# A decoder layer on one core: the order of work in the feed-forward rows, and where the first row's second stage starts

## The reference

```python
# 1: linear attention, 16 heads of 128, blocks of 64 with decay per head
qkv = silu(x @ Wqkv.T);  q, k, v = split(qkv)
out = blockwise_decayed_attention(q, k, v, slope_rate)   # = masked scores with exp(-s*(i-j))
rms = rsqrt(mean(out * out, axis=-1) + eps)              # over all heads, 2048 features
attn = sigmoid(x @ Wg.T) * (out * rms * norm_w) @ Wo.T
x1 = layernorm(x + attn)

# 2: a recurrence over the 256 steps, per feature; k = x1, v = ctx
#    y_t = (a_t + exp(u + k_t) * v_t) / (b_t + exp(u + k_t))
#    a' = exp(w) * a + exp(k_t) * v_t ;  b' = exp(w) * b + exp(k_t) ,  w = -exp(time_decay)
x2 = layernorm(x1 + y)

# 3: feed-forward with ternary weights, 512 -> 2048 -> 512
h = bitlinear(x2, w_fc); h = gelu(h); h = bitlinear(h, w_proj)
return layernorm(x2 + h)
```

## Time and profile before

| | |
|---|---|
| median of 3 runs | 1429.16 us |
| lowest to highest | 1429.12 to 1431.48 us |
| the profiled execution | 1429.61 us |
| its span (first to last instruction) | 1427.20 us |
| PE busy | 1353.2 us (95%) |
| weight load (PEld) busy | 1056.6 us (74%) |
| DVE busy | 961.6 us (67%) |
| ACT busy | 621.6 us (44%) |
| POOL busy | 268.5 us (19%) |
| mean granted clock of TensorE | 0.986 |

### The profile page before, as it was taken

The page is one execution under the profiler, slowest core; times in us unless marked ns, Lnnn a source line. Parts: engine busy times, 40 slices in busy tenths (PEclk is TensorE's granted clock), DMA queues, the critical chain, the costliest instruction groups (busy, mean ns, idle before and its releaser), DMA issues. The chain is left out here.

```text
span 1427.2 us, 21094 instructions
## 1 busy us (share of the span) xinstructions
PE 1353.2 (95%) x6898; PEld 1056.6 (74%) x6898; DVE 961.6 (67%) x1712; ACT 621.6 (44%) x1182; POOL 268.5 (19%) x199
## 2 busy tenths in 40 slices
PE   7999999998999999999999999999995789998897
PEld 6888888887888888888888888888883344454443
DVE  5666666655666657667666766555658788888873
ACT  5433434342434343433434343434331667767754
POOL 2210101110101011110101110101113454444430
PEclk9999999999999999999999999999997899999999
DMA  5011111110111010110101010000000001111000
GB/s 199 5 46 54 59 37 59 47 63 23 45 37 44 22 44 22 46 44 28 44 22 44 22 44 8 30 7 29 28 24 17 30 30 45 44 44 45 15 16 29
DMA packets 14435, 55.00 MB, mean 39 GB/s; under 512 B 2112, under 2 KB 2112, under 8 KB 12096
## 3 DMA queue, kind: packets, MB, share of 16 engines
q1 hardware_dynamic: 14400, 54.55, 11.2%
HBM read 50.35 MB, written 4.19 MB: 38 GB/s over the span
## 5 line engine op out<-in xcount | busy, mean ns | idle before, releaser
L333 PE MATMUL bank<-x_hi,w_hi 128*128 128x512 f32 x1024 | 413.3, 404 | 7.9 <-DVE x_lo L859 7.1
L335 PE MATMUL bank<-x_hi,w_lo 128*128 128x512 f32 x1024 | 401.1, 392 | 0.0
L334 PE MATMUL bank<-x_lo,w_hi 128*128 128x512 f32 x1024 | 400.1, 391 | 0.0
L844 DVE TENSOR_TENSOR resid<-resid,bank 128x512 f32<-128x512 f32 x256 | 173.6, 687 | 149.7 <-PE bank L384 148.7
L1252 POOL TENSOR_TENSOR sq_sum<-sq_sum,o_sq 128x512 f32<-128x512 f32 x64 | 104.8, 1637 | 872.2 <-ACT o_sq L604 872.2
L333 PEld LDWEIGHTS bank<-x_hi,w_hi 128*128 128x128 f32 x1024 | 193.1, 189 | 47.5 <-issue 9.1
L335 PEld LDWEIGHTS bank<-x_hi,w_lo 128*128 128x128 f32 x1024 | 192.9, 188 | 42.8
L334 PEld LDWEIGHTS bank<-x_lo,w_hi 128*128 128x128 f32 x1024 | 193.5, 189 | 36.7
L850 DVE SCALAR_TENSOR_TENSOR gated<-g_t,bank 128x512 f32<-128x512 f32 x64 | 44.0, 687 | 176.2 <-PE bank L364 176.2
L599 ACT ACTIVATE v_t<-bank 128x512 f32<-128x512 f32 x64 | 38.2, 596 | 185.9 <-PE bank L335 185.9
L382 PE MATMUL bank<-wo_hi,u_hi 128*128 128x512 f32 x256 | 100.8, 394 | 14.6 <-DVE u_lo L855 14.3
(11 more groups left out here) (147 smaller groups left out, 2401.6 us busy)
## 6 DMA issues: line engine op xcount, KB each, us to landing
w_raw<-w_ffn SPq DMA_DIRECT2D x32, 512.0 KB, 3.3
raw<-w_heads SPq DMA_DIRECT2D x15, 1024.0 KB, 4.9
raw<-w_heads SPq DMA_DIRECT2D x17, 256.0 KB, 2.7
x_in<-x_rows SPq DMA_DIRECT2D x8, 512.0 KB, 3.3
val<-ctx_t SPq DMA_DIRECT2D x8, 512.0 KB, 3.3
out<-y_out SPq DMA_DIRECT2D x8, 512.0 KB, 2.6
resid<-x_t SPq DMA_DIRECT2D x3, 1024.0 KB, 9.3
resid<-x_t SPq DMA_DIRECT2D x4, 256.0 KB, 5.2
```

Source lines behind the costliest of these rows:

```text
L333: mm(PJ[j % 2][:, :], a, c, start=kt == 0, stop=False)
L334: mm(PJ[j % 2][:, :], a, d, start=False, stop=False)
L335: last = mm(PJ[j % 2][:, :], b, c, start=False, stop=kt == KT - 1)
L844: tt(resid[:, 4 * g + t, :], resid[:, 4 * g + t, :], YB[t % 2][:, :], ALU.add).then_inc(y_added, 1)
```

## The change

On each engine the same instructions are issued, with these differences:

- In `row` DVE does both reciprocals before the aa scans, and these behind the first half-split; `input_sum` moves from the middle of the row (for row b+2) to its end (for row b+3), so that it stands ahead of the next bb scans. GpSimd does den ahead of the two products, and the root for the input norm at the row's start. `second_stats` is no longer behind `input_sum`.
- The scans have 255 columns in place of 256, over tiles of 256, since the last state was not read.
- `final` moves one unit ahead, to unit 62. In unit 63 PE turns row 0's x1 into the scores' banks, ACT copies the key and takes the exponentials between its key and value evacuations (two more table loads), DVE does the bb scans ahead of `gate(62)`, and GpSimd den and the products.
- Behind unit 63 row 0 takes the path of the others (`invert`, `fraction` on GpSimd) and `first_fraction` goes. PE does the column sums before the mix and `turn_back(0)` before the last outputs.
- The tiles of the rows lie in another order.

```diff
-            def unit(h, g, lag1=True, lag2=True, fresh=False, final=False):
+            def unit(h, g, lag1=True, lag2=True, fresh=False, final=False, turn=False):
...
                 project(h, g, K)
+                if turn:
+                    pe.wait_ge(masked, 2 * u)
+                    turn_x1(0, SC)
...
             U = UNITS
+            pe.wait_ge(key_ok, 2)
             scores(U - 1, 0)
             scores(U - 1, 1)
-            pe.wait_ge(evacuated, PROJ * U)
-            turn_x1(0)
             for tt in range(4):
                 output(HEADS - 1, U - 2, tt)
+            column_sums()
             mix(U - 1)
-            for tt in range(4):
+            pe.wait_ge(evacuated, PROJ * U)
+            turn_back(0)
+            for tt in range(2):
                 output(HEADS - 1, U - 1, tt)
+            pe.wait_ge(col_ok, 1)
+            turn_x2(0, 0)
+            for tt in range(2, 4):
+                output(HEADS - 1, U - 1, tt)
+            turn_x1(1, TR)
             pe.wait_ge(sq_added, U)
             pe.wait_ge(v_ready, U)
             square_totals(1, GROUPS)
-            column_sums()
-            turn_back(0)
-            pe.wait_ge(col_ok, 1)
-            turn_x2(0, 0)
-            turn_x1(1)
...
                     evacuate(u, j)
+                    if j == K and first_row:
+                        split_k(u)
+                        copy_key(0, SC)
+                        act.wait_ge(bias_ok, 2)
+                        exps(0)
+                        continue
...
             def row(b, first=False, next_row=True, second_row=True):
-                if next_row:
+                if second_row:
+                    root(NX, b + 2)
+                if next_row:
+                    denominator(b + 1)
                     weighted(b + 1)
-                    denominator(b + 1)
-                    numerator(b + 1)
                 if not first:
                     root(NO, b - 1)
                 if next_row:
+                    numerator(b + 1)
                     fraction(b + 1, 0)
                     fraction(b + 1, 1)
-                if second_row:
-                    root(NX, b + 2)
...
             root(NX, 0)
+            add_squares(UNITS - 3, 1)
+            pool.wait_ge(projected, PROJ * (UNITS - 1))
+            g_.memset(bb[:, :, 0:1], 1.0).then_inc(states0, 1)
+            denominator(0)
+            pool.wait_ge(wo_split, HEADS)
+            weighted(0)
             add_squares(UNITS - 2, GROUPS - 2)
-            pool.wait_ge(projected, PROJ * UNITS)
-            g_.memset(bb[:, :, 0:1], 1.0).then_inc(states0, 1)
-            weighted(0)
             numerator(0)
+            fraction(0, 0)
+            fraction(0, 1)
+            root(NX, 1)
+            second_root(0)
             add_squares(UNITS - 1, GROUPS - 1)
             rms_root(1, GROUPS)
-            second_root(0)
-            root(NX, 1)
```

More of the change, by code:

```diff
@@ L391, in square_totals, with turn_x1 @@
                 last.then_inc(sq_total, 1)
-            def unit(h, g, lag1=True, lag2=True, fresh=False, final=False):
+            def turn_x1(b, to):
+                pe.wait_ge(x1_ok, BT * b + BT)
+                wait(pe, x2_ok, BT * b)
+                for ct in range(KT):
+                    for t in range(BT):
+                        o = (ct % 2) * SEQ + t * P
+                        last = nc.tensor.transpose(to[ct // 2][:, o:o + P], x1[:, t, ct * P:(ct + 1) * P],
+                                                   ident[:, :])
+                last.then_inc(x1_turned, 1)
+            def unit(h, g, lag1=True, lag2=True, fresh=False, final=False, turn=False):
                 u = GROUPS * h + g
@@ L434, in _ @@
             for g in range(GROUPS):
[L435 to L445, removed]
+                unit(HEADS - 1, g, final=g == GROUPS - 2, turn=g == GROUPS - 1)
             def turn_back(b):
@@ L623, in copy_v, with copy_key, exps, unit @@
                 fn(v_r[:, :, :], VT[:, :].rearrange("p (a b) -> p a b", a=KT), ACT.Copy).then_inc(v_ready, 1)
-            def unit(h, g, lag1=True, split=None):
+            def copy_key(b, turned):
+                act.wait_ge(x1_turned, b + 1)
+                wait(act, r_ok, 2 * b)
+                for c in range(2):
+                    fn(key[:, 2 * c:2 * c + 2, :], turned[c][:, :].rearrange("p (a b) -> p a b", a=2),
+                       ACT.Copy).then_inc(key_ok, 1)
+            def exps(b):
+                act.wait_ge(key_ok, 2 * b + 2)
+                wait(act, num_ok, b)
+                for c in range(KT):
+                    fn(ek1[:, c, :], key[:, c, :], ACT.Exp, bias=u_neg[:, c:c + 1]).then_inc(ek1_ok, 1)
+                for c in range(KT):
+                    fn(ek2[:, c, :], key[:, c, :], ACT.Exp, bias=u_min[:, c:c + 1]).then_inc(ek2_ok, 1)
+            def unit(h, g, lag1=True, split=None, first_row=False):
                 u = GROUPS * h + g
@@ L661, in _ @@
             for g in range(GROUPS):
[L662 to L677, removed]
-                    fn(ek2[:, c, :], key[:, c, :], ACT.Exp, bias=u_min[:, c:c + 1]).then_inc(ek2_ok, 1)
+                unit(HEADS - 1, g, first_row=g == GROUPS - 1)
             def split_x2(b):
@@ L914, in head @@
                 for g in range(GROUPS):
-                    unit(h, g, final=last and g == GROUPS - 1)
+                    unit(h, g, final=last and g == GROUPS - 2, first_row=last and g == GROUPS - 1)
                     if g == 1:
@@ L1186, in _ @@
             gate(U - 1)
-            first_fraction()
+            scale_columns()
+            input_sum(1)
+            second_stats(0)
+            root = second_shift(0)
+            shift(NX, 1)
+            fc_scale(0, root)
+            for t in range(2):
+                add_y(U - 1, (U - 1) % GROUPS, t)
+            split_x2(0)
             for t in range(2, 4):
@@ L1266, in _ @@
                         cut_decay(h + 1)
-            for g in range(GROUPS - 2):
-                add_squares(GROUPS * (HEADS - 1) + g, g)
+            add_squares(GROUPS * (HEADS - 1), 0)
             def rms_root(g0, g1):
```

95 lines of the change are left out of this document (40 added, 55 removed).

## The result

| | before | changed |
|---|---|---|
| median, us | 1429.14 (1428.08 to 1431.48, 4 runs) | 1439.67 (1438.41 to 1440.93, 4 runs) |
| ratio | | 1.0073, 95% interval 1.0060 to 1.0086 |
| profiled execution: span, time, us | 1427.2, 1429.61 | 1438.9, 1440.93 |
| mean granted clock | 0.986 | 0.980 |

The changed kernel is slower by 0.73%.

The account below looks back on a forecast made before the run. The prediction took each row to be a ring of waits whose length counts, not PE's busy time. Handover -3.4, five rows +7.5 and row 6 -0.8 gave +3.3 us on 1429.16, so 1432.5; range 1425 to 1440.

Parts of the forecast that it names:

- The likeliest case: The prediction's own sum for the whole kernel: +3.3 us, so 1432.5 us; chance 0.45.
- rival A: Clock falls where each row's result is turned: +1 to +1.5 us a row, 1437.5 to 1440 us; chance 0.17.
- the point: The single forecast time of the changed kernel, 1432.5 us.
- Step 1: Row, DVE: input_sum (3.33 us) goes ahead of the bb scans, which start at 1196.5 instead of 1193.61.
- Step 2: Row, DVE: four bb scans run free in 2.35 us; GpSimd's root beside them costs 0.4; end 1199.25.
- Steps 3 and 4: Row: den 2.18, y_out done 1202.15, reciprocals done 1210.35, aa scans 1212.7, second half-split 1213.3; PE gains 0.9 us.
- Step 5: Row, GpSimd: num and four fractions follow the aa scans, 7.5 us, ending 1220.2; PE waits some 2.9 us.
- Step 6: Row, PE: turning the result takes 0.95 us, statistics start 1221.3 instead of 1219.85; a row 1.5 us longer.
- The sixth stretch: Into row 6 there is no input_sum, so the result is ready 0.8 us earlier: -0.8 us.
- the handover: From attention to the rows: row 0's second statistics at 1139.0 instead of 1142.40, -3.4 us, bounds -1 and -6.
- Rival B: GpSimd's serial tail in the rows is shorter, with a free root and handover near -6: about 1425 us; chance 0.18.
- C: Rows about even (+0.6 each) because aa and the fractions overlap, or ordering does nothing: 1428 us; chance 0.20.

Follow-up runs that it names:

- e3_filler: The changed kernel with twelve spare matmuls of 512 columns on PE just before it waits for GpSimd's last fraction; 1435.59 us.
- e1_mid_sum: The changed kernel with DVE's input_sum back in the middle of the row and GpSimd's root for it behind the fractions; 1426.01 us.
- e4_rows_old: The changed kernel with its new handover but the old order of the rows on DVE and GpSimd; 1426.25 us, ratio 0.9984.
- e7_rows_new: The kernel before with its old handover and only the new order of the rows on DVE and GpSimd; 1440.68 us, ratio 1.0077.
- e8_aa_only: The changed kernel with the aa scans between the two reciprocals instead of behind them; 1417.35 us, ratio 0.9916.

## Why the prediction was right, point by point

The range and the direction were right, and so was the mechanism of the rows: the scans become free, and a serial tail on GpSimd makes the row longer. The likeliest case was not what happened: rival A was, and it had 0.17. With most of the clock's cost gone (e3_filler) the time is 1435.59, 3.1 above the point. That the measured time is still inside the range is partly luck, since the rows are forecast well because small errors cancel, and the clock's cost falls for less than half in the rows for which rival A gave it.

**Step 1, input_sum ahead of the scans**: right. The scans start 15.47 us after the second statistics (1197.48 - 1182.01); the prediction's 1196.5 - 1181.04 is the same. e1_mid_sum shows the price.

**Step 2, the scans are free**: right, all 32 between 660 and 691 ns where the earlier trace rows had 658 to 2777. The root's 0.4 was not there: it started at 1197.60 beside the scans and took 1.06 instead of 0.70, so GpSimd waited, and DVE's four scans stayed at 2.42. The prediction read a full 0.7 for DVE out of the Trainium skill ("SBUF — State Buffer", section "Who interferes with whom") and took 0.4 itself, but the same section says that the order of issue decides who blocks. The trace agrees as far as it goes: DVE's first scan started 0.12 us before the root, and GpSimd waited. The root, which ended at 1198.66, didn't lengthen the second scan either (0.66). What the trace does show on DVE's side is the opposite case: the two small nshift instructions at 1214.05, of two columns each, took 1.96 us together beside num (1213.57 to 1215.92), where the same line took 0.15 in other places (at 1101.29). One of the signs of waiting was read too large: the prediction held the product's 2.71 against den's 2.18, but t2 takes 2.36 in the changed kernel with no such DVE instruction beside it, so about a third of that difference was not waiting.

**Steps 3 and 4, den, y_out, the reciprocals, the half-splits**: right to 0.3 us, with two errors that cancel in part: the root cost nothing where 0.4 was put down, and den took 2.35 and not 2.18. y_out ends 20.96 us into the row, forecast 21.1; the aa scans end 31.4 in, forecast 31.7. What PE gained at the second half-split (0.62 of wait instead of 1.58) is the forecast 0.9.

**Step 5, the serial tail of GpSimd**: right, and it is the step that the result rests on. 7.84 us from the end of the aa scans to the last fraction, forecast 7.5, the difference being num at 2.35 and the gaps between the instructions. PE's new wait is 2.92 to 2.95, forecast 2.9.

**Step 6, the turning**: 1.19 us from the fraction's end to the statistics, forecast 0.95, at the higher clock level. The prediction's sum slips here: 1220.2 + 0.95 is 1221.15, and it writes 1221.3. By its own terms a row would be 1.3 us longer and not 1.5; the slip of 0.15 happens to make up for most of the 0.24 by which 0.95 was too small. So a row at that level is 40.4 (e3_filler) against the 40.3 forecast. The sixth stretch, 37.68 there, was forecast at 37.6 (38.40 - 0.8); how the 0.8 comes out of the steps is not written down.

**What was mis-sized: the handover.** Forecast -3.4, measured -1.54 in this trace, -2.0 in e3_filler's and -2.4 in e4_rows_old, which has no input_sum(2) there. The result of row 0 is turned at 1094.89, 2.2 us earlier than forecast, but from there to the bb scans it takes 21.8 us and not 18.8. DVE in order of time:

```profile
1100.09 1.21 DVE L1088 SCALAR_TENSOR_TENSOR nshift<-mv,rstd_r 128x2 f32<-128x2 f32 x1 [1.12 <-POOL rstd_r L1283]
...
1110.75 0.17 DVE L1161 TENSOR_SCALAR rms_in<-bank 128x12 f32<-128x12 f32 x1 [3.27 <-PE bank L388]
1113.32 1.41 DVE L1024 SCALAR_TENSOR_TENSOR x<-resid,rms,x_in 128x512 f32<-128x512 f32 x2 [2.39 <-POOL rms L1273]
...
1116.65 2.42 DVE L1037 TENSOR_TENSOR_SCAN bb<-ew,ek 128x255 f32<-128x255 f32 x4
```

Of the 3.0 us, 1.1 is the small nshift, which has two SBUF operands and ends when GpSimd's add_squares (1100.02 to 1101.28) ends; and 0.85 is PE's transposes, which took 1.94 us for eight instead of 1.09, at a granted clock of 0.50. The prediction took the old durations of both. The remaining 1 us is not accounted for. That the three things at the end (square totals, root, input_sum) stand in series was right. From the scans to the second statistics it was 24.2, forecast 23.1.

**What decided the distance from the point: the clock.** Rival A said that it falls where the result is turned and costs 1 to 1.5 us a row. It fell in three of five rows there (0.9 us each), cost 2.3 in the five rows by the comparison with e3_filler, and 3.2 more in the sixth, the tail and the handover, where A had nothing. Its total, 5.5, was right for partly other places. The argument against it, that PE is nearly full before and after the wait, failed: PE was busy for 34.6 to 35.9 of some 41 us in each row, and the clock fell all the same.

The account of the span: forecast +3.3; handover +1.9 more than forecast in this trace (of which 0.5 clock), the five rows of e3_filler +1.4 more (202.85 - 193.94 = 8.9, of which 0.8 in the third row), the clock from there to the changed kernel 5.0 (2.3 + 1.5 + 1.2), the rest 0.1: 11.7.

Of the signs named in advance, the free scans and the new wait of 2 to 3.5 us came in every row. The stretch of 40 to 40.6 us came in one row of five (40.42), and in four of e3_filler's. Row 0's second statistics came at 1140.86 and not near 1139.

Rival B (the tail shorter than forecast) and C (rows even, or the ordering without effect) fall by the rows above: of B's three conditions only the free root came true, the fractions kept their 1.26; e7_rows_new rules C out without the new handover too.

## What to carry to other kernels

When an instruction is freed from contention, ask what its new place makes serial. Here 4.2 us of waits went out of each row's scans, while 3.3 us of input_sum and one reciprocal and half-split too many (3.9 us) went in ahead of an eight-microsecond chain on GpSimd. The aa scans one reciprocal earlier are worth 22 us by themselves (18 without the clock's part), with the contention still gone. Take the two things of a reordering apart before judging it: one half of this one gained 2.9 us and the other lost 11.4.

A wait of PE of 3 us in a nearly full row can cost more than itself: the matmuls behind it may run at the lower clock level. Whether it does is quickly seen by filling the wait with spare matmuls, as long as they end before the wait would: in e3_filler's third row they ended too late and held the transposes up themselves.

## What the runs showed that was not expected

- Twelve spare matmuls a row made two kernels faster: by 4.1 us (1439.67 to 1435.59) and 3.9 us (1426.01 to 1422.06). The median of the 64 transposes behind that wait fell from 417 to 273 ns in the first, from 421 to 273 in the second.
- GpSimd adds 1024 columns in 2.18 us when one operand's rows are 257 columns apart, and in 2.35 when they are 256 apart. The place of the tile made no difference in the one case tried, and no run tells why the pitch does.
- A DVE instruction of two columns, nshift, took 0.15 us, and up to about 1.9 when it came while GpSimd's num of 2.35 us was running (1.89 in e1_mid_sum, 1.96 for two in the changed kernel, in each row of the loop). Both its operands are in SBUF; that this is the reason is argued from the larger cases, not tested. Small instructions deserve a look at their operands before their size.
- In the row where DVE's loop turns over, 0.4 us of "issue" stood ahead of the scans (0.41 in the changed kernel, e3_filler and e8_aa_only) as soon as DVE had no slack there.
